# A DLRM tower kernel: the last group's MLP in two tiles instead of one group

## What is computed

```python
e = jnp.stack([tbl_0[ids[:, 0]], ..., tbl_25[ids[:, 25]]], axis=1)      # 2048 x 26 x 128
combined = jnp.concatenate([dense[:, None, :], e], axis=1)              # 27 vectors
inter = jnp.einsum('bnd,bmd->bnm', combined, combined)[:, I, J]         # 351 pairs
h = jnp.concatenate([dense, inter, dense], axis=1)
h = jnp.maximum(h @ W_top1 + b_top1, 0.0)                               # 512
h = jnp.maximum(h @ W_top2 + b_top2, 0.0)                               # 256
y = h @ W_top3                                                          # 1
```

## Time and profile before

| | us |
|---|---|
| median of 3 runs (lowest, highest) | 384.8 (383.59, 385.23) |
| the profiled execution's own time | 385.81 |
| its span, first to last instruction | 383.9 |
| PE busy in the span | 333.5 (87%) |
| POOL busy in the span | 269.4 (70%) |
| mean granted PE clock, as a share of full speed | 0.973 |

### The profile page before, as it was taken

How to read it: one execution, slowest core, us unless ns; L and a number is a source line. 1 busy time by engine, 2 the same in 40 slices (tenths; PEclk the granted TensorE clock), 3 DMA queues, 4 the chain that set the end, 5 groups by cost and what they waited for, 6 DMA issues and landing times.

```text
span 383.9 us, 13545 instructions
## 1 busy us (share of the span) xinstructions
PE 333.5 (87%) x6208; PEld 303.5 (79%) x6208; DVE 260.9 (68%) x206; ACT 169.3 (44%) x248; POOL 269.4 (70%) x277
## 2 busy tenths in 40 slices
PE   3777895949899998999899989999898989969787
PEld 2656784939898897979898879889897889859676
DVE  3999889574849865787668775777666776723322
ACT  2553563514445443545364543544354434532412
POOL 6787777777777777777777777777777777776000
PEclk9999998797999999999999999999999999997999
DMA  7996124251224322242215221341224112332020
GB/s 181 234 236 188 51 70 112 57 158 50 56 55 118 88 58 56 66 144 52 56 51 158 51 57 54 94 121 50 56 66 143 51 50 58 97 99 56 2 92 0
DMA packets 18985, 33.51 MB, mean 87 GB/s; under 512 B 5834, under 2 KB 11666, under 8 KB 18930
## 3 DMA queue, kind: packets, MB, share of 16 engines
q0 software_dynamic: 8848, 18.11, 18.2%
q1 hardware_dynamic: 10082, 14.55, 13.5%
HBM read 28.96 MB, written 3.68 MB: 85 GB/s over the span
## 4 chain that ended last, share of the span: by engine, by line
PE 40%; POOL 34%; issue 13%; DVE 7%; DMA 3%; ACT 2%; DVEq 0%; SPq 0%
POOL rows L390 34%; PE gram_ps L714 8%; PE hot_ps L684 8%; PE mlp_ps L684 8%; PE mlp_ps L720 4%; DVE one_hot L538 3%; PE transpose_ps L650 3%; PE mlp_ps L721 3%; PE mlp_ps L722 3%; DVE units L527 2%; DMA rows<-table,ids_sb 1%; PE hot_ids_ps L659 1%; PE mlp_ps L761 1%; DMA rows<-bounce 1%; DVE packed_lo L549 1%
## 5 line engine op out<-in xcount | busy, mean ns | idle before, releaser
L390 POOL DMA_INDIRECT rows<-table,ids_sb x272 | 268.5, 987 | 83.5 <-issue 80.7
L538 DVE TENSOR_TENSOR one_hot<-hot_ids_ps,row_numbers_sb 125x2048 fp32r<-125x2048 f32 x72 | 165.2, 2298 | 72.2 <-PE hot_ids_ps L659 62.7
L684 PE MATMUL hot_ps<-one_hot,table_hi 125*128 125x256 f32 x320 | 82.5, 295 | 3.4 <-issue 2.9
L684 PE MATMUL hot_ps<-one_hot,table_lo 125*128 125x256 f32 x320 | 79.6, 286 | 0.0
L684 PE MATMUL mlp_ps<-one_hot,table_hi 125*128 125x256 f32 x256 | 66.6, 297 | 11.8 <-DVE hidden_lo L569 6.4
L684 PEld LDWEIGHTS hot_ps<-one_hot,table_hi 125*128 125x128 f32 x320 | 62.1, 194 | 4.6 <-issue 4.6
L714 PE MATMUL gram_ps<-embed_t 128*27 128x27 f32 x4096 | 54.9, 195 | 11.2 <-issue 4.8
L684 PE MATMUL mlp_ps<-one_hot,table_lo 125*128 125x256 f32 x256 | 63.8, 286 | 0.0
L714 PEld LDWEIGHTS gram_ps<-embed_t 128*27 128x27 f32 x4096 | 45.0, 106 | 23.0 <-issue 15.4
L684 PEld LDWEIGHTS hot_ps<-one_hot,table_lo 125*128 125x128 f32 x320 | 62.3, 195 | 0.1
L684 PEld LDWEIGHTS mlp_ps<-one_hot,table_hi 125*128 125x128 f32 x256 | 49.9, 195 | 14.6 <-DVE one_hot L538 7.4
(11 more groups left out here) (80 smaller groups left out, 381.4 us busy)
## 6 DMA issues: line engine op xcount, KB each, us to landing
rows<-table,ids_sb POOLq DMA_INDIRECT x272
embed_t<-table SPq DMA_DIRECT2D x8, 448.0 KB
bounce<-units SPq DMA_DIRECT2D x8, 448.0 KB, 2.6
scratch<-bounce SPq DMA_DIRECT2D x7, 378.0 KB
dense_sb<-dense_t SPq DMA_DIRECT2D x8, 128.0 KB
scratch<-w SPq DMA_DIRECT2D x1, 512.0 KB, 4.8
units<-w_units SPq DMA_DIRECT2D x2, 252.0 KB
scratch<-table SPq DMA_DIRECT2D x1, 448.0 KB
```

Of the source, the lines that this page charges most:

```text
L390: nc.gpsimd.indirect_dma_start(rows[:, t2, f - 1, :], None, tables[table], bass.IndirectOffsetOnAxis(ids_sb[:, tile, table:table + 1], 0)) ...
L538: nc.vector.tensor_tensor(one_hot[:, k % RING], ids.to_broadcast([HOT_P, HOT_STEPS, GROUP]), row_numbers_sb[:, :, None].to_broadcast([HOT_ ...
L684: last = nc.tensor.matmul(hot_bank(n), table[:, n, step, :], one_hot[:, k % RING, step, :], start=(step == 0 and table is table_hi), stop= ...
```

## The change

Group 7's MLP is done for each of its two tiles apart, with 128 moving columns in each product where there were 256. The first tile's units (rounds r0 and r1) are packed as soon as both rounds are copied out, by DMAs of half the size (`pack_half`), into a layout of their own in `units`, `bounce` and `packed_hi`/`packed_lo`. A new step U0 splits them, and new steps A0 to A6 (`first_half`) do that tile's whole MLP in two PSUM banks that group 7 has no other use for (`hot_ps`, `hot_ids_ps`), behind M6. `last_mlp` then does the last tile's share, with 12 products without a reader instead of 36. In the step table, S0 moves ahead of G0, G1 comes right behind G0, M5 moves from between the last tile's two gram rounds to behind Q4, and U0 stands between those rounds. One more pair of pack DMAs is issued on SP, around the store of group 6's `y`.

```diff
-    "G0 S0 Q0 M0 Q1 G1 M1 M2 Q2 M3 D0 Q3 M4 Q4".split(),
-    "G0 M5 G1 M6".split(),
+    "S0 G0 G1 Q0 M0 Q1 M1 M2 Q2 M3 D0 Q3 M4 Q4 M5".split(),
+    "G0 U0 G1 M6 A0 A1 A2 A3 A4 A5 A6".split(),
 ]
-WARM_PRODUCTS = 36
+WARM_PRODUCTS = 12
...
-        last_packed_raw = by_chunk(rows[0:UNIT_P, 0, 0:2 * CHUNKS, :].rearrange("p c d -> p (c d)"))
+        last_packed_raw = [by_chunk(rows[0:UNIT_P, 0, h * CHUNKS:(h + 1) * CHUNKS, :].rearrange("p c d -> p (c d)"))
+                           for h in range(HALVES)]
+        last_units = units[:, 1].rearrange("p k q -> p (k q)").rearrange("p (h x) -> p h x", h=HALVES)
+        def packed_half(packed, h):
+            whole = packed[:, :, :, :].rearrange("p s c q -> p (s c q)")
+            return by_chunk(whole[:, h * CHUNKS * P:(h + 1) * CHUNKS * P])
...
             if g == GROUPS - 1 and 2 <= m < H1_CHUNKS:
-                return gram_ps[:, m % 2, 0:GROUP]
+                return gram_ps[:, m % 2, 0:P]
+            if g == GROUPS - 1:
+                return mlp_ps[:, m % 2, 0:P]
             return mlp_ps[:, m % 2, 0:GROUP]
+        def half_bank(m):
+            return (hot_ps, hot_ids_ps)[m % 2][:, 0:P]
...
+            def pack_half(h):
+                place = bounce.rearrange("p x -> (p x)")[h * P * HALF_UNITS:(h + 1) * P * HALF_UNITS].rearrange("(p x) -> p x", x=HALF_UNITS)
+                sp.wait_ge(early_copied, ROUNDS * (GROUPS - 1) + TILE_ROUNDS * (h + 1))
+                sp.dma_start(place, last_units[:, h]).then_inc(units_stored, 16)
+                sp.wait_ge(units_stored, 16 * (GROUPS + h))
+                by_row = place.rearrange("(s n) x -> s (n x)", s=BLOCK)[:, 0:N * HALF_UNITS]
+                sp.dma_start(last_packed_raw[h].rearrange("p s c q -> p s (c q)"),
                              by_row.rearrange("s (p x) -> p s x", p=UNIT_P)).then_inc(units_packed, 16)
...
+            sp.wait_ge(units_packed, 16 * (GROUPS - 1))
+            pack_half(0)
             store_y(GROUPS - 2)
-            sp.wait_ge(units_packed, 16 * (GROUPS - 1))
-            pack(GROUPS - 1, 1, last_packed_raw)
+            pack_half(1)
+            sp.wait_ge(half_copied, MLP_USES)
...
+            def half_copy(m):
+                act.wait_ge(half_ready, m + 1)
+                src = half_bank(m)
+                if m < H1_CHUNKS:
+                    nc.scalar.activation(hidden1_hi[:, m, half_columns(0)], src, ACT.Relu).then_inc(half_copied, 1)
+                elif m < H1_CHUNKS + H2_CHUNKS:
+                    c = m - H1_CHUNKS
+                    nc.scalar.activation(hidden2[c][:, half_columns(0)].rearrange("p (q s) -> p s q", s=BLOCK),
+                                         src.rearrange("p (s q) -> p s q", s=BLOCK),
+                                         ACT.Relu, bias=b2_sb[:, c:c + 1]).then_inc(half_copied, 1)
+                else:
+                    act.wait_ge(y_stored[(GROUPS - 1) % 2], 16 * ((GROUPS - 1) // 2))
+                    nc.scalar.copy(y_sb[0:1, (GROUPS - 1) % 2, half_columns(0)], src[0:1, :]).then_inc(half_copied, 1)
...
+            def half_units_upper():
+                act.wait_ge(units_packed, 16 * GROUPS)
+                nc.scalar.copy(packed_half(packed_hi, 0)[0:UNIT_P], last_packed_raw[0]).then_inc(units_hi, 1)
...
-            act.wait_ge(units_packed, 16 * GROUPS)
+            act.wait_ge(units_packed, 16 * (GROUPS + 1))
             for c in range(CHUNKS):
-                nc.scalar.copy(packed_hi[0:UNIT_P, :, c, :], last_packed_raw[:, :, c, :]).then_inc(last_units_hi, 1)
+                nc.scalar.copy(packed_half(packed_hi, 1)[0:UNIT_P, :, c, :], last_packed_raw[1][:, :, c, :]).then_inc(last_units_hi, 1)
...
+            def half_hidden1_lower(m):
+                dve.wait_ge(half_copied, m + 1)
+                columns = half_columns(0)
+                nc.vector.scalar_tensor_tensor(hidden1_lo[:, m, columns], half_bank(m), 0.0, hidden1_hi[:, m, columns].bitcast(F32),
+                                               ALU.max, ALU.subtract).then_inc(half_split, 1)
...
+            def half_units_lower():
+                dve.wait_ge(units_hi, GROUPS)
+                lower(last_packed_raw[0], packed_half(packed_hi, 0)[0:UNIT_P], packed_half(packed_lo, 0)[0:UNIT_P]).then_inc(units_lo, 1)
...
+            def first_half(m):
+                out = half_bank(m)
+                g, columns = GROUPS - 1, half_columns(0)
+                if m >= 2:
+                    pe.wait_ge(half_copied, m if m == MLP_USES - 1 else m - 1)
+                if 2 <= m < H1_CHUNKS + 2:
+                    pe.wait_ge(half_split, min(m, H1_CHUNKS) if m >= H1_CHUNKS else m - 1)
+                if m < H1_CHUNKS:
+                    h = slice(m * P, (m + 1) * P)
+                    if m == 0:
+                        pe.wait_ge(dense_split_lo, g + 1)
+                        pe.wait_ge(units_lo, g + 1)
+                    three_products(out, (w1d_hi[:, h], w1d_lo[:, h]), (dense_half(dense_hi, 0), dense_half(dense_lo, 0)), True, False)
+                    for c in range(CHUNKS):
+                        last = three_products(out, (w1u_hi[0:unit_p(c), c, h], w1u_lo[0:unit_p(c), c, h]),
+                                              (packed_half(packed_hi, 0)[0:unit_p(c), :, c, :], packed_half(packed_lo, 0)[0:unit_p(c), :, c, :]),
+                                              False, c == CHUNKS - 1)
+                elif m < H1_CHUNKS + H2_CHUNKS:
+                    h = slice((m - H1_CHUNKS) * P, (m - H1_CHUNKS + 1) * P)
+                    for c in range(H1_CHUNKS):
+                        last = three_products(out, (w2_hi[:, c, h], w2_lo[:, c, h]),
+                                              (hidden1_hi[:, c, columns], hidden1_lo[:, c, columns]), c == 0, c == H1_CHUNKS - 1)
+                else:
+                    for c in range(H2_CHUNKS):
+                        last = nc.tensor.matmul(out[0:1, :], w3_sb[:, c:c + 1], hidden2[c][:, columns],
+                                                start=(c == 0), stop=(c == H2_CHUNKS - 1))
+                last.then_inc(half_ready, 1)
...
             def last_mlp():
-                g = GROUPS - 1
+                g, columns = GROUPS - 1, half_columns(1)
...
-                    three_products(mlp_bank(g, m), (w1d_hi[:, h], w1d_lo[:, h]), (dense_hi[:, :, :], dense_lo[:, :, :]), True, False)
+                    three_products(mlp_bank(g, m), (w1d_hi[:, h], w1d_lo[:, h]), (dense_half(dense_hi, 1), dense_half(dense_lo, 1)), True, False)
```

More of the change, by code:

```diff
@@ L80 @@
 GROUP_BLOCKS = GROUP // BLOCK
+HALVES = TILES
+HALF_BLOCKS = GROUP_BLOCKS // HALVES
+HALF_UNITS = UNITS * HALF_BLOCKS
 ROUND_BLOCKS = 16
@@ L454, in late_columns @@
                 act.wait_ge(gram_ready, ROUNDS * g + r + 1)
-                nc.scalar.copy(unit_slot(buf, r, 0, UNITS), gram_slot(r, HALF, N)).then_inc(late_copied, 1)
+                nc.scalar.copy(unit_slot(g, buf, r, 0, UNITS), gram_slot(r, HALF, N)).then_inc(late_copied, 1)
             def hot_copy(g, k, buf):
@@ L586, in group @@
                             hidden1_lower(g - 1, n)
+                        elif step == "A" and n < H1_CHUNKS:
+                            half_hidden1_lower(n)
+                        elif step == "U":
+                            half_units_lower()
                         elif step == "W" and not mlp_before and n < len(pieces) - 1:
@@ L806, in last_mlp @@
                 pe.wait_ge(mlp_copied, MLP_USES * g + H1_CHUNKS + 2)
-                nc.tensor.matmul(out, w3_sb[:, 0:1], hidden2[0], start=True, stop=False)
+                nc.tensor.matmul(out, w3_sb[:, 0:1], hidden2[0][:, columns], start=True, stop=False)
                 pe.wait_ge(last_hidden2, 1)
-                nc.tensor.matmul(out, w3_sb[:, 1:2], hidden2[1], start=False, stop=True).then_inc(mlp_ready, 1)
+                nc.tensor.matmul(out, w3_sb[:, 1:2], hidden2[1][:, columns], start=False, stop=True).then_inc(mlp_ready, 1)
             def group(g, buf, steps, first=False):
```

42 lines of the change are left out of this document (32 added, 10 removed).

## The result

The changed kernel takes 395.57 us (median of 4 runs, 392.98 to 399.91), the kernel before on the same chip 385.01 (4 runs, 383.59 to 385.36). The ratio is 1.026, with a 95% interval of 1.020 to 1.032. So the change loses 10.6 us where the forecast had 1.6. The profiled execution took 392.98 us.

The account below looks back on a forecast made before the run. PE was taken as the bound, apart from a wait for a DRAM round trip (1.34 us idle). M6 ending 3.4 us earlier and the added products summed to 144p - 15.6 = +1.6 us on 384.8: 386.4 us, range 377 to 389.

Parts of the forecast that it names:

- p: PE's time between starts of successive 128-column products, taken as 0.119 us; the whole difference was 144p - 15.6 us.
- the head: From r0's start to M6's end: forecast 21.97 us, against 25.37 before.
- Columns set the slot: Rival for the 128-column products: moving columns set their pace, 0.060 us each, total 377.9 us; chance 0.26.
- the slot grows: Rival for the 128-column products: they fall to plain fp32's pace, 0.21 us each, total 400 us; chance 0.18.
- So PE is at Q4 at 353.5, if the clock holds: First tile's rounds, then 13 transposes and 60 products, 8.5 us, put PE at Q4 before the gather's limit of 355.45.
- for r1 I take r0's pace, 1.9 us, to 345.0: First tile's second gram round: directly behind r0, it would take 1.9 us and end at 345.0.
- a falling clock as a rival: Clock drops after 344 for as long as before; Q4 1.4 us late, loss 3.0 us, total 387.8; chance 0.14.
- The gain of 1.97 us: First tile's rounds side by side with S0 ahead: r2 starts at 357.42, 1.97 us earlier, held only by the gather.
- M5 out, 1.43 us hidden: M5 behind Q4 runs during ACT's copy; r2's start to M6's end shrinks from 5.72 to 4.29 us.
- With two stalls as long as r0's, about 1.9 more: Last tile's gram rounds: a side case in which instruction issue stalls would make M6 end about 1.9 us later.
- The tail: From M6's end to the end of the `y` copy: forecast 22.25 us, against 17.27 before.
- 72p + 2.18: A0 to A6 on PE behind M6: 72 products plus 2.18 us for two handovers and the third layer.

Follow-up runs that it names:

- run 9: The kernel before with S0 ahead of G0 and the last group's units packed tile by tile, MLP whole: 382.69 us, ratio 0.994.
- run 1: The kernel before with the change's new order of steps alone, MLP of the last group left whole: 385.3 us, ratio 1.002.
- run 7: The kernel before with S0 ahead of G0 and nothing else: 382.91 us, ratio 0.997.
- run 6: The kernel before with the new order, plus 12 products without a reader between r2 and r3: 385.45 us, ratio 1.000.
- run 2: The change with the order of steps of before, so the MLP by tiles alone: 392.61 us, ratio 1.019.
- run 8: The kernel before with the last group's units packed tile by tile, MLP whole at 256 columns, 32 products without a reader: 384.04 us, ratio 0.998.
- run 3: The change with all 144 products of the two tiles taking their 128 columns twice: 390.95 us, ratio 1.015.
- run 11: The change with only the A steps' products taking their columns twice: 390.62 us, ratio 1.013.
- run 4: The change with 7 products without a reader ahead of A4 and 7 ahead of A6: 400.42 us.
- run 10: The change with all tile products' columns taken twice, S0 first, rounds apart, M5 between the last rounds, no products without a reader: 388.19 us, ratio 1.006.
- run 5: The change without A0 to A6, with 36 products without a reader, in the order of steps of before: 383.31 us, ratio 0.997.

## Why the prediction was wrong

The forecast was a loss of 1.6 us and the measured one is 10.6. Two steps failed. The sum took all of 144p at the full clock and put a low clock in the A steps at nothing; it cost some 4.5 us in the profiled execution and more in others. And the head was to be 3.4 us shorter; it was 0.75 shorter.

**The slot, right.** All was said to depend on p. It was taken as 0.119 with 0.107 as the low end, because the weight load sets it; it is 0.111 to 0.112. Half the columns save 7% of the slot. "Columns set the slot" (chance 0.26) and "the slot grows" (0.18) are both out: the time of 400 that the latter gave was met by some runs, by luck and for another cause. The Trainium skill (TensorE: Matmul & The Clock Gate, section LDWEIGHTS) makes a load its columns over 1.2 GHz, 0.107 for 128, which is near the measured slot at the full clock. At the lower clock the slot with the same load is 0.213, so by this trace the rule doesn't hold there; the measured slot decides.

**"So PE is at Q4 at 353.5, if the clock holds", wrong.** The sum's first term had PE there 1.95 us ahead of the gather. It came at 356.40, though r0 had started 0.56 earlier: 3.5 us late. The step that failed is "for r1 I take r0's pace, 1.9 us, to 345.0": the rounds ended at 346.3, with stops of 1.63 and 1.77 in place of one of 1.37, which is 2.0 us; and the clock then fell (0.92 and 0.65 in two windows), which is 1.7 us of full-speed time. I had allowed a second stop of up to 1.9 us as free, and a falling clock as a rival (0.14), but not both at once. Against 1.95 us of slack either alone would nearly be hidden (for the stops that is an estimate from these numbers): with one stop and the same cost of the clock, run 9 has a head of 23.59. The gain of 1.97 us is not in run 1, and it is in run 7, where only S0 moved.

**"M5 out, 1.43 us hidden", wrong.** Taking M5 out of the gram instructions left a stop of the same length in its place (2.19 us against 2.26), and run 6 shows that such a stop takes in work. From r2's start to M6's end the forecast had 4.29 us; it was 5.37 in the change and 5.07 in run 1, against 5.72 before, and 5.17, 5.26 and 5.27 in runs 2, 8 and 9, which kept M5 there. So the move gave nothing that these didn't have. "With two stalls as long as r0's, about 1.9 more" was a side remark where it should have been the term. Together with Q4 this is the head: 3.4 us of gain forecast, 0.75 measured.

**The tail's sizes, right; its clock, wrong.** With the clock up the terms are good to some 0.2 us (run 2) or 0.3 (run 3: 22.59 against 22.25). What failed is the step from "72p + 2.18" to a time, with p at the full clock all through. In the change 10.2 us at the lower clock cost what stands between 25.74 and 21.2, some 4.5 us, and 7 more in the worse execution. My clock rival looked at the stretch after 344 alone. I took the clock in the A steps for granted, because PE would be busy there. That the A steps' 128 columns make it fall is borne out by the pair of run 11 and the change: the same instructions in the same order, with 72 products wider, 388.3 to 391.2 us against 393.0 to 400.9 in eight runs (393.8 to 400.9 in the four on the same chip). Whether the clock falls in the A steps (the change) or just before (run 4), with narrow products behind it stayed down for 10, 26 and 27 us. With mostly 256-column products behind the fall it was back after 3.4 us (run 10; the stretch after 344 in the change) to 6.8 us (the same stretch before and in run 3). It is a tendency and no law: run 2 had the same narrow A steps, with the clock at 1.00 in its profiled execution, and its other three runs took 391.6 to 401.4. The Trainium skill (TensorE: Matmul & The Clock Gate, section Why this matters for your kernels) advises, for matmuls with a thin M, to keep the K-tiles together or to pad M, against a clock that oscillates. In this case it was the moving columns that were thin, and no wait was over 0.8 us in the A steps; padding these columns from 128 to 256 cost 0.008 us a product and kept the clock (runs 3 and 11).

**What the numbers add up to.** From head and tail, 2.65 + 4.5 - 144 x 0.007 (the smaller slot) = 6.1 us above the forecast's +1.6 gives +7.7. The profiled executions differ by 392.98 - 385.81 = 7.2, and the rest is r0's start, 0.56 earlier. The median of the change stands 2.6 us above its profiled execution, and that of the kernel before 0.8 below its own, which makes 10.6. The change's other executions have a lower mean granted clock, 0.948 to 0.957 against 0.969, so in them the low clock lasted longer.

**The direction.** It came out as forecast, in part by luck: with the measured slot my sum is 144 x 0.112 - 15.6 = +0.5 us, so two thirds of the forecast loss came from a slot taken too large. Even without the clock falling in the A steps the change loses: run 3 loses 6.3 us and run 10 2.9. The wait that it removes was 1.34 us of idle PE and 24 products without a reader (24 x 0.119 = 2.9 us), and for it PE does 72 products (8.0 us) and two handovers more. (My "84 products" counted the last tile's 12 dense ones, which were there before.)

**Open.** Why the clock falls or stays down under narrow products right behind r2 and r3, and not under those at the end of runs 5 and 11, which follow wide products, nor in run 2's profiled execution; and why it came back at 381.5 in one execution of the change and not at all in the other.

## What to carry to other kernels

Where a product's slot hardly depends on its columns (0.119 us with 256, 0.112 with 128), splitting such work in two to hide a wait nearly doubles it, so the wait has to be longer than the second half. The transfers can be split by themselves with the products left whole, though half the bytes saved only 1.1 of 5.9 us (run 8). Work between two bursts of tiny instructions may be free there, and moving it out then gained nothing here; look at the idle time put down to issue, not only at waits on data.
